# Shared expert first in the first expert layer, and another order of the prologue

## The reference

```
x = x + ga * attention(layernorm(x) * (1 + ca) + sa)          # layer 0: 16 heads, latent k and v, causal
x = x + gb * ffn0(layernorm(x) * (1 + cb) + sb)
x = x + ga1 * recurrent(layernorm(x) * (1 + ca1) + sa1)       # layer 1: gated scan and a gated MLP
x = x + gb1 * ffn1(layernorm(x) * (1 + cb1) + sb1)

def ffn0(x):                                                  # 8 experts and one shared, 128 -> 512 -> 128
    p = softmax(x @ router_w.T + router_b)                    # top 2 of 8, their p normalised to sum 1
    return shared(x) + sum_e comb[:, e] * expert_e(x)         # each: gelu(x @ w1.T + b1) @ w2.T + b2
```

## Time and profile before

| | us |
|---|---|
| median of three runs | 677.3 (677.08 to 679.79) |
| profiled execution, its own time | 679.79 |
| its span, first to last instruction | 678.0 |
| PE, DVE, ACT, POOL busy | 606.8, 545.4, 486.1, 173.3 |
| mean granted PE clock, of full speed | 0.949 |

### The profile page before, as it was taken

One profiled execution on the slowest core, in us unless ns is written; L12 is line 12 of the kernel. 1 busy time (PEld: TensorE's weight loads), 2 busy tenths in 40 slices (PEclk: granted clock), 3 DMA queues, 4 the chain that ended last, 5 costly groups with the idle time before them and its releaser, 6 DMA issues.

```text
span 678.0 us, 11084 instructions
## 1 busy us (share of the span) xinstructions
PE 606.8 (89%) x3284; PEld 441.1 (65%) x3284; DVE 545.4 (80%) x1345; ACT 486.1 (72%) x857; POOL 173.3 (26%) x147
## 2 busy tenths in 40 slices
PE   8788889888997899999999999782699899999996
PEld 5355556555545568888888887351385788888884
DVE  3667888888866658878888887756899689999997
ACT  4548999999553669999999998677635466666663
POOL 3422223332301415443554443310143000000000
PEclk9789999999996899999999999976699799999999
DMA  7000000000100120122202220000000042222201
GB/s 239 1 0 2 2 2 0 0 0 0 32 1 0 48 113 37 57 95 94 91 2 93 93 85 1 23 1 0 0 1 0 1 150 87 87 86 86 86 1 62
DMA packets 6651, 29.85 MB, mean 44 GB/s; under 512 B 887, under 2 KB 1024, under 8 KB 4417
## 3 DMA queue, kind: packets, MB, share of 16 engines
q1 hardware_dynamic: 6610, 29.37, 12.2%
HBM read 28.18 MB, written 1.19 MB: 43 GB/s over the span
## 4 chain that ended last, share of the span: by engine, by line
PE 62%; DVE 26%; issue 5%; ACT 5%; DMA 1%; SPq 0%; POOL 0%; DVEq 0%; ACTq 0%; POOLq 0%
PE PS L1127 16%; PE PS L1129 16%; PE PS L1128 16%; DVE STAT L802 8%; PE PS L1273 2%; DVE RA L822 2%; PE PS L1228 2%; DVE HN L656 2%; PE PS L1153 2%; DMA AR<-in_wmod 1%; DVE SU L828 1%; PE PS L1242 1%; DVE HN L652 1%; ACT RA L605 1%; DVE AR L1086 1%
## 5 line engine op out<-in xcount | busy, mean ns | idle before, releaser
L937 DVE TENSOR_TENSOR RA<-AR,RA 128x512 fp32r<-128x512 f32 x140 | 134.3, 983 | 29.1 <-ACT RA L509 28.4
L508 ACT ACTIVATE AR<-PS,BI 128x512 f32<-128x512 f32 x144 | 99.4, 691 | 26.2 <-PE PS L1129 16.6
L1127 PE MATMUL PS<-HH,WH 128*128 128x512 f32 x272 | 109.5, 403 | 0.1
L1129 PE MATMUL PS<-HL,WH 128*128 128x512 f32 x272 | 107.4, 395 | 0.0
L1128 PE MATMUL PS<-HH,WL 128*128 128x512 f32 x272 | 107.3, 395 | 0.0
L509 ACT ACTIVATE RA<-PS,BI 128x512 fp32r<-128x512 f32 x144 | 98.4, 683 | 0.0
L802 DVE CUSTOM_DVE_ANT_0 STAT<-PS,MQ 128x128 f32<-128x128 f32 (+1 forms) x256 | 76.3, 354 | 20.2 <-PE PS L1229 20.1
L1127 PE MATMUL PS<-RA,WH 128*128 128x512 f32 x208 | 82.4, 396 | 2.5 <-DVE RA L1093 2.1
L1129 PE MATMUL PS<-RA,WH 128*128 128x512 f32 x208 | 81.2, 391 | 0.0
L1128 PE MATMUL PS<-RA,WL 128*128 128x512 f32 x208 | 81.2, 390 | 0.0
L312 POOL TENSOR_TENSOR AR<-AR 128x512 f32<-128x512 f32 x32 | 51.2, 1601 | 111.9 <-DVE AR L756 111.9
(11 more groups left out here) (196 smaller groups left out, 1185.1 us busy)
## 6 DMA issues: line engine op xcount, KB each, us to landing
AR<-comb SPq DMA_DIRECT2D x16, 1024.0 KB, 4.6
WS<-in_w SPq DMA_DIRECT2D x9, 512.0 KB, 5.6
WS<-in_w SPq DMA_DIRECT2D x8, 384.0 KB, 3.1
M<-in_mats SPq DMA_DIRECT2D x1, 1384.0 KB, 12.2
X<-in_xT SPq DMA_DIRECT2D x4, 256.0 KB, 4.8
out_xT<-X SPq DMA_DIRECT2D x4, 256.0 KB, 2.1
AR<-in_wmod SPq DMA_DIRECT2D x1, 768.0 KB, 9.2
KM<-in_kmats SPq DMA_DIRECT2D x1, 162.5 KB
```

The source lines that it names most:

```text
L508: act.activation(G[:, c, :], PS[:, c, :], ACT.Gelu_apprx_tanh, bias=bias).then_inc(s["act"], 1)
L937: dve.tensor_tensor(out=GL[:, m0 % 2, c, :], in0=G[:, c, :], in1=f(GH[:, m0 % 2, c, :]), op=ALU.subtract).then_inc(s["lo"], 1)
L1127: pe.matmul(out, wh, xh, start=first, stop=False)
L1129: return pe.matmul(out, wh, xl, start=False, stop=last)
```

## The change

1. **Prologue.** PE first computes only the two vectors that the first norm needs (two thin matmuls into bank 6), then `variance(0,2)` and `variance(0,3)`, then all 24 thin matmuls. DVE copies two vectors, normalises all four blocks, and takes the rest of the modulation after that. GpSimd's `LH` waits until the first norm is done (`hn_done` 8); `LL` moves behind `join(7)` into the attention loop.
2. **Expert order.** The shared expert is expert 0 of the visits and runs before the gates exist. Its result is copied to `ACC` (`keep0`), the bias product is added (`add_bias`), and routed experts are scaled from visit 4 on. The last expert is now a routed one: `residual_last` scales first.
3. **Overlap.** The first visit begins when block 0 is normed. Block 3's mean, variance and norm and the four `router` calls stand between chunks of visits 0 and 1. Block 3's inverse root goes another way: variances as a column (4 matmuls of one column), eps added on ACT, power -0.5 on GpSimd (128x4), and spread over a bank by 4 matmuls. `route` for this layer becomes 20 small DVE instructions dealt out between the low parts of visits 1 to 4, without softmax; GpSimd takes e to a power (128x16).
4. **GpSimd** splits both first experts' weights at the end of attention, and DVE makes visit 0's low parts.
5. **Loops** of this layer are written out (no `Fori`), and the biases are read in place, so the small `BI` copies go.

The core of the diff (declarations, index arithmetic and the SP queue's rewritten but equal order are left out):

```diff
 GpSimd
+            gp.wait_ge(hn_done, 8)
             gp.tensor_scalar(LH[:, :], lm, 1.0, 0.0, ALU.mult, ALU.add).then_inc(l1_split, 1)
-            gp.wait_ge(l1_split, 1)
-            gp.tensor_tensor(out=LL[:, :], in0=lm, in1=f(LH[:, :]), op=ALU.subtract).then_inc(l1_split, 1)
...
             for n in range(UNITS):
                 if n + 3 < UNITS:
                     join(n + 3)
-            gp.wait_ge(moe[0]["w_in"], 16)
-            split_weights(0, 0, 0, 1024)
-            for t in range(NBLK):
+                if n == 4:
+                    gp.wait_ge(l1_split, 1)
+                    gp.tensor_tensor(out=LL[:, :], in0=lm, in1=f(LH[:, :]), op=ALU.subtract).then_inc(l1_split, 1)
+            next_weights(0)
+            next_weights(1)
+            for t in range(3):
                 split_hidden(1, HN, t)
-            for c in range(4):
-                gp.wait_ge(moe[0]["act"], 2 * (c + 1))
-                gp.tensor_tensor(out=GL[:, 0, c, :], in0=G[:, c, :], in1=f(GH[:, 0, c, :]), op=ALU.subtract)\
-                  .then_inc(moe[0]["lo"], 1)
-            gp.wait_ge(moe[0]["w_in"], 32)
-            split_weights(0, 1, 1, 1024)
-            experts(0, E0, 1024)
+            gp.wait_ge(const_done, 6)
+            gp.wait_ge(ve_done, 1)
+            gp.tensor_tensor(out=RS[:, :], in0=VE[:, :], in1=CON[:, 3:4].to_broadcast([128, 4]), op=ALU.pow)\
+              .then_inc(root_done, 1)
+            split_hidden(1, HN, 3)
+            gp.wait_ge(moe[0]["rstep"], 11)
+            gp.tensor_tensor(out=ODDS[:, :], in0=CON[:, 4:5].to_broadcast([128, 16]), in1=RM["den"][:, :], op=ALU.pow)\
+              .then_inc(odds_done, 1)
+            next_weights(2)
+            gp.wait_ge(moe[0]["acc_init"], 4)
...
 ScalarE
+            gelu0(0, 0)
+            gelu0(0, 1)
             square(1, XC, 3)
-            inverse(1, 3)
-            router_exp(0)
+            gelu0(0, 2)
+            biased_variance()
+            gelu0(0, 3)
+            for m in range(1, 4 * E0):
...
 VectorE, prologue
+            divide_by_root(0, 0)
+            dve.wait_ge(mod_first, 1)
+            ... copies of two vectors
+            modulate(0, 0)
+            for t in range(1, NBLK):
+                normalise(0, t)
             dve.wait_ge(mod_psum, 1)
             ... the rest of the modulation and the gates
-            for t in range(NBLK):
-                normalise(0, t)
 VectorE, expert layer
             normalise(1, 0)
             normalise(1, 1)
+            rest(1, HN, 0)
             attended(3)
+            rest(1, HN, 1)
             normalise(1, 2)
-            rest(1, HN, 0)
-            rest(1, HN, 1)
             centre(1, 3)
             rest(1, HN, 2)
-            normalise(1, 3)
-            rest(1, HN, 3)
-            route(0, E0)
...
+            lower0(0)
+            lower0(1, (nothing, lambda: normalise(1, 3), lambda: rest(1, HN, 3), largest))
+            lower0(2, (first_equal, first_chosen, second_largest, second_equal))
+            lower0(3, (second_chosen, nothing, nothing, nothing))
+            keep0(0)
+            keep0(1)
+            lower0(4, (shares, weigh_chosen, combine, nothing))
+            keep0(2)
+            lower0(5, (nothing, lambda: keep0(3), lambda: rows_in(0), lambda: rows_in(1)))
+            lower0(6, (lambda: rows_in(2), lambda: rows_in(3), nothing, lambda: add_bias(0)))
+            lower0(7, (lambda: add_bias(1), nothing, nothing, lambda: add_bias(2)))
+            add_bias(3)
+            scale0(4)
+            for m in range(7, 32):
+                lower0(m + 1)
+                scale0(m - 2)
...
+            def residual_last(t):
+                m = visits.index((E0 - 1, t))
+                scale0(m)
                 dve.wait_ge(x_part, t + 1)
-                    in0=PS[:, 4 + t, ...]
+                    in0=YW[:, m % 2, ...]
 TensorE, prologue
+            for i in range(2):
+                mm = pe.matmul(PS[:, 6, 8 * i:8 * i + 8], WMOD[:, 128 * i:128 * i + 128], SC[:, 0:8], start=True, stop=True)
+            mm.then_inc(mod_first, 1)
+            variance(0, 2)
+            variance(0, 3)
             ... 24 thin matmuls
-            variance(0, 2)
-            variance(0, 3)
 TensorE, expert layer
-            pe.wait_ge(ot_done, UNITS)
-            router(0, 0)
-            router(0, 1)
-            mean(1, 3)
-            router(0, 2)
-            variance(1, 3)
-            router(0, 3)
...
+            for c in range(4):
+                hidden0(0, c)
+                if c == 1:
+                    mean(1, 3)
+            step0(0, between=routers_between)       # router 0, variance(1,3), router 1, router 2
+            step0(1, between=last_router_between)   # spread_root after c 0, router 3 after c 2
+            step0(2)
+            step0(3)
+            step0(4, between=routes_between)        # after c 0 and c 1 wait for kept 3, 4; route_out(c)
+            step0(5, between=biases_between)        # bias_out(0), (1) after c 2, 3
+            step0(6, between=last_biases_between)   # bias_out(2), (3) after c 1, 3
+            for m in range(7, 34):
+                step0(m)
```

More of the change, by code:

```diff
@@ L1 @@
+import math
 import concourse.bass as bass
@@ L196, in variance_bank @@
                 return 4 + t
+            if (k, t) == (1, 3):
+                return 6
             return 6 + t % 2 if k == 4 else 4 + norm_at(k, t) % 2
+        visits = [(k, t) for k in range(E0) for t in range(NBLK)]
         def split_at(k):
@@ new lines, in _, with weights0, gates0 @@
+            s0 = moe[0]
+            def weights0(k):
+                if k > 0:
+                    sp.wait_ge(s0["split"], 2 * k)
+                sp.dma_start(WS[:, 0:1024], w0[k, :, :]).then_inc(s0["w_in"], 16)
+            def gates0(k):
+                if k >= 3:
+                    sp.wait_ge(s0["ymul"], 4 * (k - 2))
+                sp.dma_start(WB[:, (k - 1) % 2, :], comb0[k - 1:k, :].to_broadcast([128, TOK]))\
+                  .then_inc(s0[f"wb_in{(k - 1) % 2}"], 16)
+            for k in range(3):
+                weights0(k)
@@ new lines, in _, with weights1, gates1 @@
+            sp.wait_ge(s0["ct"], 4)
+            sp.dma_start(comb0, CT[0:E0, :]).then_inc(s0["stored"], 16)
+            sp.wait_ge(s0["stored"], 16)
+            gates0(1)
+            gates0(2)
+            for k in range(3, E0):
+                weights0(k)
+                gates0(k)
+            s1 = moe[1]
+            def weights1(e):
+                sp.wait_ge(s1["split"], 2 * e)
+                sp.dma_start(WS[:, 0:768], w1[e, :, :]).then_inc(s1["w_in"], 16)
+            def gates1(e):
+                if e >= 2:
+                    sp.wait_ge(s1["ymul"], 8 * (e - 1))
+                sp.dma_start(WB[:, e % 2, :], comb1[e:e + 1, :].to_broadcast([128, TOK]))\
+                  .then_inc(s1[f"wb_in{e % 2}"], 16)
@@ L242, in _ @@
+            sp.wait_ge(s0["split"], 2 * E0)
+            sp.dma_start(WS[:, 0:768], w1[0, :, :]).then_inc(s1["w_in"], 16)
+            weights1(1)
+            sp.wait_ge(s1["ct"], 4)
+            sp.dma_start(comb1, CT[0:E1, :]).then_inc(s1["stored"], 16)
+            sp.wait_ge(s1["stored"], 16)
+            gates1(1)
+            for e in range(2, E1):
+                weights1(e)
+                gates1(e)
             for t in range(NBLK):
@@ L516, in _ @@
-            act.activation(BI[:, 0, :], V[:, VAT["b1"]:VAT["b1"] + 4], ACT.Copy).then_inc(bias_done, 1)
-            for m in range(8):
-                gelus(m, m, m // 4)
-            with act.Fori(1, 4) as it:
-                for u in range(8):
-                    gelus(8 * it + u, 8 + u, 2 * it + u // 4)
-            for m in range(32, 36):
-                gelus(m, m, 8)
+                    gelu0(m, c)
             square(2, XC, 0)
@@ L1144, in variance @@
                 pe.wait_ge(sq_done, at + 1)
+                if (k, t) == (1, 3):
+                    pe.wait_ge(cen_done, 8)
+                    for i in range(4):
+                        mm = pe.matmul(PS[:, 6, i:i + 1], STAT[:, BLK * t + 128 * i:BLK * t + 128 * i + 128],
+                                       OND[:, 0:1], start=True, stop=True)
+                    mm.then_inc(var_done, 1)
+                    return
                 if k == 1 and t == 0:
@@ L1387, in output0, with step0 @@
                 if c == 3:
                     mm.then_inc(s["y"], 1)
-            def step0(m, m0, e_next, ahead=True, between=None):
-                if ahead and m0 % 4 == 3:
-                    pe.wait_ge(s["split"], 2 * e_next + 2)
+            def step0(m, between=None):
+                if m % 4 == 3 and m + 1 < len(visits):
+                    pe.wait_ge(s["split"], 2 * visits[m + 1][0] + 2)
                 for c in range(4):
-                    if ahead:
-                        hidden0(m + 1, m0 + 1, c)
-                    output0(m, m0, c)
+                    if m + 1 < len(visits):
+                        hidden0(m + 1, c)
+                    output0(m, c)
```

439 lines of the change are left out of this document (246 added, 193 removed).

## The result

| | before | after |
|---|---|---|
| median, us | 678.1 (677.1 to 679.8, 4 runs) | 734.4 (730.8 to 736.9, 4 runs) |
| ratio, 95% interval | 1 | 1.082 (1.079 to 1.086) |
| profiled execution: time / span | 679.8 / 678.0 | 736.2 / 734.4 |
| mean granted TensorE clock | 0.949 | 0.849 |

What follows compares the result with a forecast made beforehand. TensorE (62% of the span) and VectorE (26%) were taken to bound the kernel. Terms -3.4 + 4.0 - 4.2 + 2.4 = -1.2 us gave 676 us from the median of 677.3, range 670 to 681.5.

Steps and rivals of the forecast that it cites:

- term 2: Attention: `LL` on GpSimd holds DVE's cast and later small subtractions; +4.0 us, bounds 1.0 and 4.5.
- term 3: Front of the expert layer: TensorE begins step 7 earlier, at 266.6 instead of 270.8 after 9.0 of waits; -4.2 us.
- Term 1: Prologue: last latent projection ends at 25.7 instead of 29.1, DVE no longer blocked by `LH` and `LL`; -3.4 us (1.7 to 6.9).
- fourth rival: Prologue: clock stays low through the projections, gain only 1.7, about 678 us; a third of the forecast's chance (0.44).
- Term 4: Tail: four scalings of the last expert's output on DVE ahead of the residuals; +2.4 us, bounds 1.4 and 2.8.
- that kind of contention: Rival: GpSimd's long instructions hold DVE's chain in all their new places; 4.7 us above forecast, about 681; chance 0.14.
- Nothing: No effect from written-out loops, `BI` copies, SP's order, or attention's second split (up to 2 us if it meets the chain).

Runs made afterwards that it cites:

- e8: Changed kernel with TensorE's attention loop written out and sixteen unused 512-column matmuls in the pause behind `LL`; 682.4 us (one run).
- e3: Changed kernel with TensorE's attention loop written out and a burst of twelve unused 512-column matmuls once, at unit 12; 699.3 us (one run).
- e5: Kernel before with only the changed kernel's prologue, `LL` right behind `LH`, FFN as before; 676.7 us, ratio 0.9973.
- e1: Changed kernel with `LL` put back in the prologue right behind `LH`; 679.5 us, ratio 1.0029.
- e13: Changed kernel with `LL` behind `LH`, thin modulation products dealt out, layer 1's weight splits behind the third norm's block splits; 674.3 us, ratio 0.9948.
- e7: Changed kernel with `LL` in the middle of the first FFN and layer 1's weight splits behind the third norm's block splits; 677.6 us, ratio 0.9981.
- e9: Kernel before with the new prologue, `LL` behind `LH`, and the thin modulation products dealt out between `variance` calls; 673.8 us, ratio 0.9938.
- e14: Kernel before with the new prologue, `LL` behind `LH`, thin products dealt out, the same code measured again beside another run; 674.2 us, ratio 0.9937.
- e2: Kernel before with only `LL` moved into the attention loop behind `join(7)`; 733.3 us (one run).

## Why the prediction was wrong

**The step that failed is the price of term 2.** I wrote that `LL` makes the cast wait 3.4 us and the subtraction 1.1, took 4.0 for it, bounded it at 4.5, and said that "the loop has no slack there". Measured: the two were held for 3.7 us together, and TensorE was idle for 3.45. The mechanism of the wait and its size were right, and the sum was still wrong by 58 us, 56 of them here, because I priced the wait as time that passes once. What the runs showed in its place is a second effect of the same wait: TensorE idle in it loses its clock (e8 against `after`), and this loop doesn't win it back by itself (e3), so that each of the 24 units left is 2.34 us longer.

I had the warning in the rows. The clock fell behind a thin stretch in the prologue and came back behind the latent projections, and the five microseconds at half clock at 209 to 219 stand in my own term 3. I used the clock for the stage in which I saw it move and never asked of attention: what does this loop run at if the clock falls here, and what in it would lift it again? Half of the answer could have been worked out: TensorE busy 53 of 60 at full clock has no room for longer matmuls, so TensorE becomes the bound if the clock stays low. That it does stay low in this loop no row before showed; the `keep_clock` matmuls in the kernel hinted at it.

The Trainium skill, TensorE: Matmul & The Clock Gate, section Part 1, has sustained matmul activity release the throttle, and its section HAM oscillation has idle gaps bring it back. The trace agrees with the second (3.45 us idle, clock 0.50 from 70 us on). With the first it does not agree as it stands: in attention TensorE was busy 60.00 of 60.00 us and stayed at 0.50, and the measurement decides. What about these matmuls leaves the clock down is not settled by these runs; shown is only that twelve of 512 columns brought it back (e3).

**Term 1** (-3.4, last projection at 25.7): right in place and size at the projections, with 25.2 as the median of ten traces, 3.9 saved. But the whole kernel gained only 1.8 us (e5: 0.27%). In e5's trace a lead of 4.1 us at the projections is 2.6 at attention's end; its dip of the clock at 30 to 38 is longer than that of the kernel before at 38 to 44. My fourth rival, that the clock stays low through the projections, happened in all ten traces to some degree, and in the three that end at 27.5 to 27.8 as it was priced.

**Term 3** (-4.2): -4.7 measured, but in part by luck. The waits of TensorE in the front sum to 5.4 us in e1's trace where I had 9.0, and the gain is only 0.5 larger, so something else in that sum was about 3 us too small. The rows account for 0.3 of it (a bias product is 1.12 us in the earlier trace rows, not 1.05); the rest was not traced. The two powers on GpSimd took 1.03 and 3.27 us, both under their cover of about 5.

**Term 4** (+2.4, bounds 1.4 to 2.8): +4.9 measured, outside the bounds. The scalings themselves cost 1.6 to 2.5 (e13, e7), as bounded. The 2 to 3 on top go with the residual pairs that the scalings push into GpSimd's split, up to 3.1 us in one execution. I listed that kind of contention as a rival and looked for it at `LL` and the splits that moved, not at DVE work that moved into a split that stayed.

**"Nothing":** holds for the loops written out (a step of the expert layer takes 5.44 us as before), but not for the second split at the end of attention: in six of eleven traces it met the chain, and TensorE waited 1.5 to 1.7 us ("up to 2" was the proviso). With terms 3 and 4 at -4.7 and +4.9 they cancel, so that without the clock the change would be about the prologue's gain, the stall and this split. e8, the changed kernel with its clock kept, took 682 where I said 676. Its trace against that of the kernel before, with the forecast in brackets: projections 1.7 us earlier (3.4), attention 5.4 longer (4.0), front and middle 5.2 shorter (4.2), boundary 5.8 longer (2.4), last stage 1.7 shorter (0); in all 2.6 longer, where the forecast was 1.2 shorter.

## What to carry to other kernels

- Price a wait twice: once as time, and once as idle time of TensorE. Ahead of a long loop of small matmuls that run near TensorE's limit, a pause of 3.5 us cost 56; the same pause filled with unused 512-column matmuls cost about 4 (one run). Look for stretches where the profile's clock sits at 0.50 with TensorE busy throughout: a short burst of wide matmuls there is worth trying.
- Cut a long GpSimd instruction into pieces, or put it where DVE has no chain: one of 3.7 us cost 56 us, two of 1.95 or four of 1.08 left the clock alone, though the four cost 4 us more than `LL` in the prologue.
- When DVE work is added in front of a chain, look at what of GpSimd the chain's instructions now fall beside: a scaling of 0.7 us in front pushed a pair into a split, and that cost up to 3.1 more here.

The best complete version was the kernel before with the new prologue, `LL` behind `LH`, and the thin products dealt out (e9, e14): 0.9938 and 0.9937, about 4 us under the kernel before and 60 under the changed one.

## What I had not expected of the hardware

- TensorE's clock has two lasting states under one and the same instruction stream: 4.39 us a unit at 1.00 and 6.73 at 0.50, for 160 us, until the first output projections (L1398, 512 columns).
- Being busy by the profile is not enough to raise it: 60.00 of 60.00 us at 0.50 in two kernels (`after`, e2).
- Twelve matmuls of 512 columns, 4.4 us, raised it (e3).
- Executions of one kernel differ by where the clock dips: the last projection of e9 and e14, the same code, ends at 21.47 and 24.76 us. That need not be the whole kernel's difference: their attention ends 0.36 us apart.
- Which of two instructions is held when DVE and GpSimd start within 0.05 us of each other changed between executions: 3.09 us for the DVE pair in five traces, 1.45 in three.
